# Moving the output projection of an attention tile ahead of a run of transpositions on TensorE

## The reference, cut to what matters

```python
q = (h @ wq).reshape(b, s, NH, D).transpose(0, 2, 1, 3)
k = (h @ wk).reshape(b, s, NKV, D).transpose(0, 2, 1, 3)   # repeated GROUPS = 4 times
v = (h @ wv).reshape(b, s, NKV, D).transpose(0, 2, 1, 3)   # likewise
scores = jnp.einsum('bhqd,bhkd->bhqk', q, k) / jnp.sqrt(jnp.float32(D))
scores = jnp.where(causal, scores, jnp.finfo(scores.dtype).min)
attn = jax.nn.softmax(scores, axis=-1)
out = jnp.einsum('bhqk,bhkd->bhqd', attn, v)
out = out.transpose(0, 2, 1, 3).reshape(b, s, NH * D)
return out @ wo
```

## Time and profile before

| | us |
|---|---|
| median of 3 runs | 1777.69 |
| the runs | 1776.51 to 1777.84 |
| time of the profiled execution | 1774.87 |
| its span, first to last instruction | 1772.9 |
| PE busy | 1697.7 |
| DVE busy | 1062.5 |
| ACT busy | 1056.7 |
| one sequence of 8 steps (752.61 to 822.80) | 70.19 |

### The profile page before, as it was taken

One profiled execution on the slowest core, in us unless ns is written; L12 is line 12 of the kernel. 1 busy time (PEld: TensorE's weight loads), 2 busy tenths in 40 slices (PEclk: granted clock), 3 DMA queues, 4 the chain that ended last, 5 costly groups with the idle time before them and its releaser, 6 DMA issues.

```text
span 1772.9 us, 30900 instructions
## 1 busy us (share of the span) xinstructions
PE 1697.7 (96%) x11858; PEld 1335.0 (75%) x11858; DVE 1062.5 (60%) x2724; ACT 1056.7 (60%) x2389; POOL 215.1 (12%) x262
## 2 busy tenths in 40 slices
PE   7999799999999999999999999999989999999985
PEld 5777477777777767777777777777769999898874
DVE  3777676686677776866876767668692521111124
ACT  2444677787787877877877777778773212221212
POOL 2222100000000000000000000000011222222323
PEclk9999899999999999999999999999999999999997
DMA  3000400000000000000000000000028584777693
GB/s 90 1 1 2 146 1 10 1 1 10 1 1 10 1 1 8 3 1 1 10 1 1 10 1 1 1 1 1 25 73 285 163 265 125 250 231 264 193 312 123
DMA packets 76414, 116.44 MB, mean 66 GB/s; under 512 B 10277, under 2 KB 61349, under 8 KB 76272
## 3 DMA queue, kind: packets, MB, share of 16 engines
q1 hardware_dynamic: 64944, 100.82, 16.4%
q0 software_dynamic: 7968, 11.58, 3.2%
q10 hardware_dynamic: 3360, 2.10, 0.4%
HBM read 139.48 MB, written 16.12 MB: 88 GB/s over the span
## 4 chain that ended last, share of the span: by engine, by line
PE 83%; DVE 11%; DMA 3%; ACT 2%; issue 1%; POOL 0%; ACTq 0%; POOLq 0%; DVEq 0%
PE bank L1875 13%; PE bank L1941 13%; PE wide L2030 12%; PE bank L1816 9%; PE wide L1858 7%; PE wide L1859 6%; PE bank L2040 6%; PE bank L1950 5%; PE bank L1672 3%; DVE arena L1191 3%; DVE arena L1199 3%; DVE qhl L1184 1%; DMA hbuf<-y_sb,torow 1%; PE wide L2050 1%; PE wide L1684 1%
## 5 line engine op out<-in xcount | busy, mean ns | idle before, releaser
L1191 DVE CUSTOM_DVE_ANT_0 arena<-wide,arena 128x896 f32<-128x896 f32 (+7 forms) x512 | 382.7, 755 | 238.6 <-PE wide L1859 231.2
L885 ACT ACTIVATE arena<-arena,nmax 128x896 f32<-128x896 f32 (+7 forms) x512 | 398.8, 780 | 97.4 <-DVE nmax L1191 94.7
L897 ACT COPY arena<-bank 128x512 f32<-128x512 f32 x576 | 311.7, 586 | 77.4 <-PE bank L1875 72.6
L1858 PE MATMUL wide<-khi,qhl 128*128 128x512 f32 (+3 forms) x768 | 343.6, 448 | 1.4 <-DVE vt L1174 1.3
L1875 PE MATMUL bank<-ident,arena 128*128 128x128 f32 x2304 | 308.6, 273 | 11.9 <-DVE arena L1199 8.0
L1875 PEld LDWEIGHTS bank<-ident,arena 128*128 128x128 f32 x2304 | 260.9, 140 | 39.9 <-issue 23.0
L1941 PE MATMUL bank<-arena,vt 128*64 128x256 f32 x2304 | 276.9, 385 | 1.3 <-DVE acc L1540 1.3
L1199 DVE TENSOR_SCALAR arena<-arena,rinv 128x896 f32<-128x896 f32 (+7 forms) x512 | 258.1, 525 | 9.1
L1859 PE MATMUL wide<-klo,qhl 128*128 128x512 f32 (+3 forms) x768 | 256.2, 342 | 0.0
L2030 PEld LDWEIGHTS wide<-wo,arena 128*128 128x128 f32 x2112 | 241.6, 192 | 2.8 <-issue 1.2
L2030 PE MATMUL wide<-wo,arena 128*128 128x128 f32 x2112 | 242.1, 276 | 0.0
(11 more groups left out here) (315 smaller groups left out, 1656.0 us busy)
## 6 DMA issues: line engine op xcount, KB each, us to landing
arena<-in_L_ffn_w SPq DMA_DIRECT2D x117, 1024.0 KB
ybuf<-prod SPq DMA_DIRECT2D x17, 128.0 KB, 2.2
wq_g<-in_L_ffn_wq SPq DMA_DIRECT2D x8, 256.0 KB, 2.5
wo<-in_L_ffn_wo SPq DMA_DIRECT2D x16, 128.0 KB, 3.2
xbuf<-x_all SPq DMA_DIRECT2D x1, 2048.0 KB, 7.9
hbuf<-acc SPq DMA_DIRECT2D x2, 1024.0 KB, 10.2
tbuf<-rT_all SPq DMA_DIRECT2D x4, 512.0 KB, 3.8
acc<-hbuf SPq DMA_DIRECT2D x4, 512.0 KB, 11.0
```

The lines of the kernel that those rows point to most:

```text
L885: nc.scalar.activation(probs[t % 2][:, h, 0:w], probs[t % 2][:, h, 0:w], ACT.Exp, bias=nmax[:, t % 2, h:h + 1], scale=-1.0, accum_out=rsum ...
L897: nc.scalar.copy(pT[t % 2][m], bank_of((t, m))).then_inc(S("pT_ready"), 1)
L1191: nc.vector.tensor_tensor_reduce(out=probs[t % 2][:, h, 0:w], in0=scores_of(t, h), in1=causal[:, SEQ - w:SEQ], scale=-1.0, scalar=-MASKED, ...
L1858: mm(dst, q, khi[:].rearrange("p (b c) -> p b c", c=P)[:, keys], start=True, stop=False)
```

## The change

In each step of the attention loop PE does the output projection of tile t-2 right behind the scores of head 2, ahead of the second run of transpositions of tile t-1. In the two last steps, which have no scores, it stays where it was. No instruction is added or taken away, and the streams of the other engines are the same.

```diff
                 if scored and t:
                     score(t, 2)
+                if weighing and t < TILES:
+                    project_out(t - 2)
                 if turning:
                     turn_part(t - 1, 1)
                 if t == TILES + 1:
                     turn_slot(0, 0, 16)
-                if weighing:
+                if weighing and t >= TILES:
                     project_out(t - 2)
                 if scored and t:
                     score(t, 3)
```

## The result

| | before, us | changed, us |
|---|---|---|
| median of 4 runs | 1777.1 | 1793.8 |
| the runs | 1775.1 to 1777.84 | 1790.18 to 1795.54 |
| span of the profiled execution | 1772.9 | 1791.7 |

The changed kernel takes 1.0097 times as long (95% interval 1.0085 to 1.0109); by the medians that is 16.7 us more. The forecast was 1793, with a range of 1783 to 1799.

A forecast was written before the change was run, and what follows sets the result against it. PE was taken to set the time. Losses of 6.5, 4.2 and 4.5 us sum to 15.2; the profiled 1774.87 becomes 1790.1, and with the median 2.8 above it the forecast is 1793, range 1783 to 1799.

The forecast's parts named there:

- Part 1: Steps with t % 8 = 2: PE idles until oT is copied, then the uncovered block follows; +0.43 us each, 6.5 in all.
- The statement that PE can't win it back: Steps after t % 8 = 2: their stalls (0.47 us in step 60) move along with PE, so the delay stays.
- the rival of transpositions that go ahead: Second run on PE: its transpositions pass the projection waiting for oT, so that wait costs nothing; 1786.4 us, chance 4%.
- The evidence that the prediction had for it: PE in step 60, as cited: transpositions wait 0.47 us and the ready scores behind start only after, so order is strict.
- One sign: Step 66, changed profile: the second run of transpositions should start about 0.9 us later.
- Part 2: Steps with t % 8 of 7 or 0: the item waits for ACT's later copies; +0.28 and +0.30 us, 4.2 and 4.5 in all.
- The rival in which ACT makes up its lag: ACT's copies or exponents run closer together, so only the wait for oT counts; 1784.2 us, chance 12%.
- Kinds 3 to 6: Steps with t % 8 from 3 to 6: the item waits for an earlier block, nearest slack 0.7 us; no loss.
- Part 3: PE's new neighbouring groups in some 105 steps: zero taken, bound 0.05 us each from weight loads, 5.3 us either way.
- Part 4: DVE's addition at steps with t % 8 = 0: its wait for the projection goes, with zero gain to PE.
- The sum: Whole kernel: 6.5 + 4.2 + 4.5 = 15.2 us of loss.
- the late exponents: ACT's delayed exponents 2 and 3: DVE wants them only next step, behind its maximum of head 0; no loss.

The follow-up runs named there:

- the run with the copy first: The changed kernel, with ACT copying the third run's first block ahead of exponent 2 at steps with t % 8 of 0 or 7; 1797.65 us, ratio 1.0133.

## Why the prediction was right, point by point

**Part 1, the wait for `oT`.** Forecast +0.43 a step at kind 2, measured +0.44; 6.5 us in all, against 6.6 by the steps and 5.8 by the medians of the kernel with kind 2 alone. The statement that PE can't win it back held: kinds 3 and 4 didn't change. Two details were as worked out, or nearly: the projection starts 0.05 us behind the copy, and the block didn't pass it. With that the rival of transpositions that go ahead is out. The evidence that the prediction had for it was of step 52, not 60, which changes nothing in it. One sign was put wrong: the second run of step 66 was to start about 0.9 us later, which is the projection's length without the gap that the same part of the prediction puts in front of it. It starts 3.81 us after the step's first scores instead of 2.39, 1.42 later. Nor did PE run without a gap there before: 0.14 us of waiting for DVE stood ahead of the block, and is part of the new gap, so that it adds nothing to the loss.

**Part 2, the late copies.** Forecast +0.28 at kind 7, measured +0.30. At kind 0, +0.30 was taken and +0.36 measured. The mechanism was right and the term a little small. Its parts in step 72, counted from the step's first scores (831.61 here, 822.80 before): the second run starts at 5.78 instead of 4.86, so 0.92 later and not 0.86, which fits the weight load's 0.05 that was counted only in part. On ACT the three copies and the exponent take 1.84 (838.02 to 839.86) instead of the 1.42 and 0.40 that were added up, and the third run's first copy starts at 8.25 instead of 7.90. The item's weight load follows the copy's end by 0.05, as before: 0.35 of the 0.36 us. The rival in which ACT makes up its lag is out, since kinds 0 and 7 alone cost 10.3 us.

**Kinds 3 to 6.** Forecast zero, measured 0.1 us in the timed run with these kinds alone (interval -1.8 to 1.4). The slack of 0.7 us was measured as 0.75.

**Part 3, the neighbours on PE.** Zero was taken, with 5.3 us either way as the bound. Zero had no better reason than that both groups ran at their own rate in one step. The run with kinds 3 to 6 has 60 such steps and no change, so the bound was much wider than the thing; kind 0 has about 0.05 us of it, behind its short scores.

**Part 4.** DVE lost most of its wait for the projection (21.5 us to 9.1), and no step became shorter by it.

**The sum.** 15.2 us were forecast, 16.7 measured. By the steps, 15 sequences of 1.08 us make 16.2. The mechanisms were right, and their terms 1 us too small in sum, for the most part at kind 0 (15 x 0.06). That the forecast 1793 lies within 1 us of the measured 1793.8 is a little luck: the median that it started from, 1777.7, was 0.6 above the one that a fourth run gave, and that made up for part of the sum's 1.5. The spans of the two profiles stand further apart, 18.8 us. From the start of step 121 to the last projection the changed kernel took 87.6 us instead of 83.6; that isn't in the sum, and the next section but one shows the same order without it.

**The rest.** Where the experiments failed was not in the reading of the change but in a repair: in the run with the copy first, the price of ACT's idle time ahead of two exponents of 1.15 us was not looked for one step on. The prediction had said of the late exponents that DVE wants them only in the next step. For the lag of 0.28 us that was enough: exponent 3 ends 1.77 us into the next step with the change as before it. With the repair it ends at 2.89, and it wasn't.

## What to carry to other kernels

When an operation is moved ahead on the engine that sets the time, look first at when its input is made: work that stood in front of it may have been covering just that wait, and an engine that runs its stream in order pays the wait and then the work. Then follow what was pushed back to the engine that consumes it, and look for the first place where the bound engine waits for a result behind it; where it has slack the push is free, and where it is already limited there each part of the lag counts. The same move is a gain where there is an idle gap and the input can be made early, so it is worth deciding per step kind, and each repair on the other engine has to be followed into the next step.

## What the runs showed of the hardware that was not expected

In the changed kernel's profile the last sequence holds a stretch with a mean granted clock of 0.57, that is, most of it at the lower of the two levels (1.2 GHz; the upper is 2.4); a window of 8 us and those around it, columns as above:

```profile
1280.00:1296.00 16.00, 13.84 (x87) 10.20 (x85) 12.03 (x33) 12.63 (x39) 0.00 (x0) 1.00 0.03 9
1296.00:1304.00 8.00, 8.00 (x39) 6.26 (x39) 3.14 (x17) 2.24 (x8) 1.63 (x1) 0.57 0.01 2
1304.00:1328.00 24.00, 21.24 (x154) 17.30 (x153) 22.89 (x89) 17.52 (x37) 0.00 (x0) 1.00 0.07 23
```

In this profile the clock falls while PE runs the router's 32 matmuls of 8 columns (line 1890, from 1293.59), which took 4.58 us here and 3.64 in the profile of before, where the clock stayed at 1.00 in this place:

```profile
1280.00:1288.00 8.00, 8.00 (x63) 7.08 (x62) 5.34 (x35) 4.19 (x13) 1.63 (x1) 1.00 0.01 3
```

It isn't tied to the change. The kernel with kinds 3 to 6 moved, as fast as before, has 0.79 in the same stretch:

```profile
1280.00:1288.00 8.00, 8.00 (x48) 6.37 (x48) 4.91 (x34) 3.22 (x9) 1.64 (x1) 0.79 0.01 3
```

and that with only the last sequence moved ran at 1773 to 1775 us eight times of eleven and at 1779.1 to 1779.2 three times, with a mean clock of 0.983 to 0.985 instead of 0.986 or 0.987; where in these three the clock fell isn't recorded. Nor does the order bring it each time. The kernel with the first block of the third run copied ahead has the changed order in the last sequence too, and its clock stays at the upper level from the start of step 121 to that of step 127:

```profile
1275.18:1333.53 58.35, 50.79 (x353) 38.76 (x351) 45.58 (x163) 41.00 (x104) 2.85 (x3) 1.00 0.08 28
```

There, from the start of step 121 to the last projection, it takes 83.4 us, as long as the kernel before (83.6), where the changed kernel took 87.6. So by this profile the order itself costs nothing in the last sequence. A dip in it comes in some executions and not in others, and a single pair of profiles can differ by 4 us in this stage for it. What decides whether it comes was not tested; nor was it tested whether the change makes it more frequent, and the three late runs of eleven leave that open.
